# Newton's steps, a convolution half and a load moved in a fused convolution and expert kernel

## The reference, cut to what matters

```
n  = layernorm over channels of x                       # first norm
x2 = x + relu(bn2(conv2(sign(relu(bn1(conv1(sign(n))))))) + n)
t  = x2 as 16384 tokens of 64 values
u  = layernorm over channels of t                       # second norm
logits = u @ gate_w + gate_b ; the two best of 16 experts, softmax over both
y  = sum over the two experts of weight * (silu(u@w1) * (u@w2)) @ w3
out = t + y, back as images
```

## Time and profile before

| | us |
|---|---|
| median of 3 runs | 516.52 |
| lowest, highest | 514.38, 517.49 |
| profiled execution | 519.35 |
| its span, first to last instruction | 517.5 |
| PE busy | 467.4 (90%) |
| DVE busy | 436.1 (84%) |
| ACT busy | 398.7 (77%) |
| POOL busy | 291.7 (56%) |
| mean granted TensorE clock | 0.93 of 2.4 GHz |

### The profile page before, as it was taken

The page is one execution under the profiler, slowest core; times in us unless marked ns, Lnnn a source line. Parts: engine busy times, 40 slices in busy tenths (PEclk is TensorE's granted clock), DMA queues, the critical chain, the costliest instruction groups (busy, mean ns, idle before and its releaser), DMA issues.

```text
span 517.5 us, 14217 instructions
## 1 busy us (share of the span) xinstructions
PE 467.4 (90%) x4186; PEld 417.1 (81%) x4186; DVE 436.1 (84%) x1240; ACT 398.7 (77%) x946; POOL 291.7 (56%) x380
## 2 busy tenths in 40 slices
PE   7989999999996453999999999999999999999981
PEld 6657767686774432899999999999999999999971
DVE  3676886887978988899999999999999899999982
ACT  4777888786965321699989989998999889989860
POOL 3200007777777787677766666666454545555562
PEclk9789889898998765799999999999999999999996
DMA  6971012022000003330132222242332524310054
GB/s 170 290 306 42 0 42 70 29 71 67 32 30 30 30 23 90 88 78 32 39 81 64 64 49 54 65 100 62 99 98 48 135 57 127 103 36 18 19 169 162
DMA packets 62664, 40.97 MB, mean 79 GB/s; under 512 B 50003, under 2 KB 54318, under 8 KB 62080
## 3 DMA queue, kind: packets, MB, share of 16 engines
q1 hardware_dynamic: 52784, 29.30, 21.9%
q0 software_dynamic: 8800, 8.94, 5.2%
q10 hardware_dynamic: 1008, 1.84, 1.0%
HBM read 21.46 MB, written 19.19 MB: 79 GB/s over the span
## 4 chain that ended last, share of the span: by engine, by line
PE 75%; DVE 15%; issue 4%; DMA 3%; ACT 2%; POOL 1%; POOLq 0%; DVEq 0%; SPq 0%; ACTq 0%
PE up L974 16%; PE up L976 13%; PE turn L987 12%; PE up L805 8%; PE lines L1006 6%; PE small L821 3%; PE small L850 3%; PE small L955 3%; PE lines L1008 3%; DMA x_in<-in_x 2%; PE up L780 2%; PE up L791 1%; DVE match L1275 1%; PE small L1017 1%; PE turn L833 1%
## 5 line engine op out<-in xcount | busy, mean ns | idle before, releaser
L527 POOL DMA_INDIRECT results<-result,page_in x147 | 153.7, 1045 | 106.8 <-ACT xc L706 66.2
L506 POOL DMA_INDIRECT pages<-payload,slot_int x128 | 129.6, 1013 | 101.4 <-DVE slot_int L1414 60.4
L974 PE MATMUL up<-up_w,xs_hi 128*128 x588 | 160.7, 306 | 2.8 <-DVE xs_lo L1513 2.4
L976 PE MATMUL up<-up_w,xs_lo 128*128 x588 | 148.0, 284 | 0.0
L974 PEld LDWEIGHTS up<-up_w,xs_hi 128*128 128x128 f32 x588 | 112.6, 192 | 5.4 <-issue 3.8
L706 ACT ACTIVATE xc<-up 128x512 f32<-128x512 f32 x147 | 90.8, 618 | 30.1 <-PE up L976 30.0
L976 PEld LDWEIGHTS up<-up_w,xs_lo 128*128 128x128 f32 x588 | 113.4, 193 | 0.0
L1589 DVE SCALAR_TENSOR_TENSOR hidden<-up,page_in,xc 128x128 f32<-128x128 f32 x196 | 59.3, 344 | 13.9 <-ACT xc L706 13.6
L1599 DVE TENSOR_TENSOR hidden_lo<-turn,hidden_hi 128x512 f16<-128x512 f32 x98 | 67.3, 687 | 0.0
L719 ACT ACTIVATE hidden_hi<-turn 128x512 f16<-128x512 f32 x98 | 62.7, 639 | 0.0
L987 PE MATMUL turn<-ident,hidden 128*128 128x128 f32 x392 | 58.8, 273 | 0.0
(11 more groups left out here) (262 smaller groups left out, 971.2 us busy)
## 6 DMA issues: line engine op xcount, KB each, us to landing
pages<-x SPq DMA_DIRECT2D x4, 1332.0 KB, 11.5
page_in<-pages SPq DMA_DIRECT2D x147, 36.0 KB
page_in<-pages SPq DMA_DIRECT2D x147, 32.0 KB
x_in<-in_x SPq DMA_DIRECT2D x7, 512.0 KB, 3.4
out<-up_raw SPq DMA_DIRECT2D x5, 512.0 KB, 3.1
results<-result,page_in POOLq DMA_INDIRECT x147
up_raw<-in_L_ffn_w SPq DMA_DIRECT2D x4, 512.0 KB, 7.7
pages<-payload,slot_int POOLq DMA_INDIRECT x128, 2.2
```

Of the source, the lines that this page charges most:

```text
L506: pool.indirect_dma_start(out=pages, out_offset=bass.IndirectOffsetOnAxis(ap=slot_int[q % PAYLOADS][:, t:t + 1], axis=0), in_=payload[q % ...
L527: pool.indirect_dma_start(out=results, out_offset=bass.IndirectOffsetOnAxis(ap=page_in[g % LOADS][:, k, D + AT_TOKEN:D + AT_TOKEN + 1].bit ...
L974: pe.matmul(target, xs_hi[g % 2][:, k * P:(k + 1) * P], weights[:, bass.ds(e * 2, 2 * HID)], start=True, stop=False)
L976: last = pe.matmul(target, xs_lo[g % 2][:, k * P:(k + 1) * P], weights[:, bass.ds(e * 2, 2 * HID)], start=False, stop=True)
```

## The change

Three edits. On SP, the load of pair 2 is issued ahead of the four transfers of blank rows, and so ahead of the wait for the cleared memory; before, it stood behind them. On PE, the first half of the first convolution of pair a stands in front of `center2` half 0 of pair s instead of behind it. On DVE, `newton_slack` and `newton_sum` of the second norm of pair b move out of `second_choice` into `slots`, which gets `b` for that; only in pass 3, which has no `slots`, they stay where they were. `newton_root` stays in `second_choice`.

```diff
             sp.dma_start(down_raw[:, :, :], ffn_w3.rearrange("e h d -> h e d")).then_inc(down_in, 16)
+            load(2)
             sp.wait_ge(blank_made, 2)
             for part in range(4):
                 sp.dma_start(pages.rearrange("(p part r) w -> part p r w", p=P, part=4)[part], blank)\
                     .then_inc(blanked, 16)
-            for q in range(2, PAIRS):
+            for q in range(3, PAIRS):
                 load(q)
...
+                if a < PAIRS:
+                    conv(0, 0, a)
                 if 0 <= s < PAIRS:
                     center2(0, s)
                 if a < PAIRS:
-                    conv(0, 0, a)
                     for c in range(CH):
                         norm(c, a)
...
                 then(dve.tensor_reduce(best[:, 1, :], logits[:, :, :], AX.X, ALU.max))
-                if b < PAIRS:
+                if r == 0:
                     newton_slack(1, b)
                 settled()
                 matches(1)
-                if b < PAIRS:
+                if r == 0:
                     newton_sum(1, b)
-                else:
-                    settled(1)
+                settled(1)
                 dve.tensor_tensor(gap[:, :], best[:, 0, :], best[:, 1, :], ALU.subtract).then_inc(gap_ready, 1)
...
-            def slots(q):
+            def slots(q, b):
...
                 then(dve.tensor_tensor(base_new[:, :], offset[:, :], full[:, :], ALU.add))
+                if b < PAIRS:
+                    newton_slack(1, b)
                 settled(1)
...
                 then(dve.tensor_tensor(rank_old[:, :, :], rank_old[:, :, :], rank, ALU.add))
+                if b < PAIRS:
+                    newton_sum(1, b)
                 settled(1)
...
-                    slots(z)
+                    slots(z, b)
```

## The result

Over 20 runs of each, the changed kernel took 513.51 us in the median and the kernel before 518.56; the ratio is 0.9881, 95% interval 0.9854 to 0.9907, so 1.2% faster. Everything that the change touches lies in the first stage, and that stage gained 13.5 us: the first product of the page stage starts at 193.17 instead of 206.69.

The account below looks back on a forecast made before the run. PE and DVE handing over bound the first stage's passes, with POOL's scatter queue behind: 9.3 us earlier, capped at 6.2, less 1.7 for the clock, gives 4.5 off the 516.52 median, 512.0 us; range 507.0 to 515.5.

Parts of the forecast that it names:

- The load: Third pair's load ahead of the blank rows: removes PE's 1.04 us idle, gain 1.0 us, bounds 0 and 1.0.
- The forecast `center` at 36.2: Sign to look for on PE: `center` of the third pair at about 36.2 us.
- The swap: First convolution half ahead of `center2` on PE: 0 taken, bounds 0 and 1.4 us once a pass.
- Newton's steps: Steps within `slots`, passes 4 to 9: 1.8 us each in passes 5 to 7, 1.6 in pass 8, 1.3 in 9.
- the forecast of no wait there: Sign to look for: PE without a wait in front of `gate` in passes 5 to 9, here pass 9.
- Pass 4's stall: DVE's slack waits for ACT's guess; `slots` loses 1.3 us plus 0.1, POOL's first scatter comes 0.4 us later.
- rival 3: PE idles before the norms, clock falls, late guess makes the slack wait in every pass: 514.7 us, chance 0.14.
- The queue: POOL's 128 scatters start 0.4 us later, lose 2.6 us of waits, so end only 2.2 us earlier.
- the cap: At the ninth page group PE can pass at most 6.2 us earlier (5.2 to 6.4), 4.0 + 2.2.
- The stall and its price: PE waits 3.1 us for the ninth page group; the clock's fall behind it costs 1.7 us, bounds 0 and 3.
- Rivals 1 and 2: 1: queue limits but stall is cheap, 510.3 us, chance 0.22; 2: queue does not hold PE, 507.2 us, chance 0.10.
- Rival 4: Slower: POOL's scatters stretch beside a denser DVE, 0.13 us each, 528.6 us; chance 0.06.

Follow-up runs that it names:

- swap: First convolution half put in front of the second centring, nothing else, against the kernel before: ratio 0.9990.
- + ninth result buffer: The kernel before with a ninth result buffer in the dead tile of the raw convolution weights, without the change: ratio 1.0039.
- Newton: Only Newton's steps moved from `second_choice` into `slots`, load and convolution as before, against the kernel before: ratio 0.9975.
- Newton, buffer: Only Newton's steps moved into `slots`, plus a ninth result buffer, against the kernel before: ratio 0.9961.
- Newton, swap: The whole change without the earlier load of the third pair, no ninth buffer, against the kernel before: ratio 0.9971.
- the ninth buffer: The changed kernel with nine instead of eight page and result buffers: ratio 0.9734 to the kernel before.

## Why the prediction was right, and where only its sum was

512.0 us forecast, 513.51 measured, inside the range; faster by 1.2%, a case that had 0.40 where "within 1%" had 0.53. The frame held: shorter passes, a queue of scatters that doesn't follow, a stall at the ninth group, and a price in the clock. But two terms were far too small, those of the load and of Newton's steps with the swap.

1. **The load was mis-sized: 1.0 us taken, with 1.0 as the upper bound; 4.2 measured** at pass 2's `gate` in these two profiles (39.07 to 34.83), and 1.2 to 1.4% alone. The step that failed is "not more, since PE has no other gap there". The gap was read in one execution. A wait is the difference of two times, and only one of them stands still: in all seven profiles without the edit the third pair's `center` starts between 37.2 and 38.0 us, when the load behind the blank rows has landed, with waits of 1.03 to 4.70 us ("swap" and "+ ninth result buffer" left out). TensorE's arrival is what varies. In the execution that I read, the clock stood at 0.50 from 12 to 16 us and at 0.73 from 16 to 20, 3.1 us of full clock lost, and TensorE came late enough to hide most of the load. With the edit, `center` starts at 31.5 to 36.8 in seven profiles, never with a wait. Pass 2's `gate` comes at 35.97 in the mean of these seven, and at 40.48 in that of five without it (the kernel before, twice, "Newton", "Newton, buffer" and "Newton, swap"). The forecast `center` at 36.2 was wrong with it. The row to doubt was the earlier trace rows: 11.36 us against 3.4 for a load whose end no engine's pace could move.

2. **The swap, 0 taken: right alone, wrong in company.** I named the very wait it would cover and then put it at 0, "because the norms behind both still wait for ACT's widened roots". They do wait in the change (0.49 to 0.79 us; before it TensorE had no wait there), but the clock stays at 1.00 behind these waits, while behind 0.91 us in front of the second centring it fell. Worth 3.6 to 5.1 us with Newton's steps.

3. **Newton's steps: the mechanism right, the size one of a pair.** With the swap, the gates of passes 5, 6, 7 and 8 follow one another 2.2, 2.0 and 3.8 us faster than before (18.33, 18.56, 16.81 against 20.54, 20.53, 20.62), so 1.8 each was low. Without the swap the first two give 0.55 and 0.25: the 1.8 each is not theirs alone. From pass 4's `gate` to pass 9's the steps and the swap gain 11.4 us (101.8 to 90.4), against 8.3 taken; the steps without the swap 6.0 to 8.1 (95.8, 95.7 and 93.8). All passes gain only 9.9, because the way from pass 3's `gate` to pass 4's, which Newton's steps don't shorten, took 22.47 us instead of 20.80; it is 22.5 to 22.7 in five of the 14 profiles and 20.8 in the others, with and without each edit. In pass 9 I read VectorE's 1.32 us and missed the 7.01 us of TensorE's own wait for the slack; 2.53 of it are left, and the forecast of no wait there was wrong.

4. **Pass 4's stall: 1.3 us taken, 1.60 measured**, and no other pass has it, against rival 3, of which only the wait in front of the norms came, without a fall of the clock. That it delays the queue by 0.4 us is not shown: without the stall the queue ends no sooner.

5. **The queue: right.** By the forecast it lost 2.6 us of waits, and both of them are gone; from the first scatter to the last it took 167.25 us instead of 169.96, 2.7 less. But its start moved with the load: the last scatter is at 241.21, not 244.3, and the ninth group's last load is issued at 254.07, not 257.1. That raised the cap from 6.2 to 9.5 us. That load landed 2.1 us after its issue (254.07 to 256.17), where 2.4 were taken. The 6.2 is rounded up: its own rows give a margin of 3.9 us (6.3 - 2.4) and a cap of 6.1, with bounds of 5.1 and 6.3.

6. **The stall and its price: right.** 3.1 us forecast, 3.46 measured; 1.7 us of clock forecast, 1.7 measured, and the ninth buffer gives 5.4 back. Rivals 1 and 2 fall with these two numbers.

7. **Rival 4 falls.** The median scatter takes 959 ns where it took 958, and all 128 together 129.5 us where they took 129.6, beside a VectorE whose listed waits between 95 and 170 us fell from 11.8 to 3.2 us. The Trainium skill ("SBUF — State Buffer", section "SBUF: two separate sides") would have some VectorE instructions hold GpSimd's reads; the few long scatters that could look like it (2.48 and 1.74 us, and 2.90 and 1.76 before) are no more than before, and the trace does not bear the rule out as a cost of the change.

So the sum of the first stage was 9.3 and came to 13.5; the cap was 6.2 and came to 9.5; the price of 1.7 stood. By profiles the change is worth 7.4 us where 4.5 were forecast; by medians, 5.05, by the ratio some 6.2 (0.0119 of 518.56). That the time came out within 1.5 us is partly luck. The queue took back only 0.9 of the 4.2 us that I missed in the first stage; 3.3 were still missed at the ninth group. The profiled execution of the change lies 1.6 us below its median and that of the kernel before 0.8 above, which is the 2.4 between 7.4 and 5.05. And the forecast started from a median of 516.52 of three runs, where 20 gave 518.56; the same 4.5 off that would have been 514.1.

## What to carry to other kernels

Before a wait is priced, ask which of its two ends is pinned and which varies: a load behind 5 MB of stores landed at 37.2 to 38.0 us here whatever TensorE had done until then, and one profile shows only how late the engine happened to be. Move a step that ends one wait, and look for the next operation of the same engine that needs the same partner; independent work put in front of that one can be worth nothing alone and everything together. A short wait ahead of TensorE's work is to be priced with the slow products that may follow it, and where the wait can't be removed, it can be filled.

## What the runs showed of the hardware that was not expected

- The clock's first fall is chance: with the same instructions up to there, "Newton" has 0.50 and 0.74 in 12 to 16 and 16 to 20 us, "Newton, buffer" 1.00 and 1.00. Up to 3 us of full clock hang on it, and a wait for a load behind it hides them.
- Most waits of 0.8 to 1.0 us in front of `gate` and of the second centring were followed by products at the 1.2 GHz level (4.45 us for 2.81, 2.71 for 1.48); those of 0.84 to 0.96 us in pass 5 of three profiles were not, nor was one of 0.79 us in front of the norms. What decides between them was not tried.
- A load of 512 KB issued behind 5.3 MB of blank rows needed 11.4 to 14.5 us in the profiles of the kernel before, "Newton" and "Newton, buffer", against 4.1 to 4.3 ahead of them.
